# Last cross attention: score products for the maximum stream 128 key columns in place of 77

## The reference

```python
q = (x @ Wq + bq).reshape(B, N, NUM_HEADS, HEAD_DIM)      # 2 x 512 x 16 x 8
k = (y @ Wk + bk).reshape(B, M, NUM_HEADS, HEAD_DIM)      # 2 x 77 x 16 x 8
v = (y @ Wv + bv).reshape(B, M, NUM_HEADS, HEAD_DIM)
scores = jnp.einsum('bnhd,bmhd->bhnm', q, k) * scale
attn = jax.nn.softmax(scores, axis=-1)
out = jnp.einsum('bhnm,bmhd->bnhd', attn, v).reshape(B, N, IMAGE_DIM)
h = jax.nn.relu(out @ W1 + b1)
return h @ W2 + b2
```

## Time and profile before

| what | value |
|---|---|
| median of 3 runs | 844.75 us |
| the three runs | 837.37, 844.75, 848.48 us |
| the profiled execution | 845.99 us |
| its span in the trace | 843.9 us |
| mean granted TensorE clock | 0.805 |

### The profile page before, as it was taken

The page is one execution under the profiler, slowest core; times in us unless marked ns, Lnnn a source line. Parts: engine busy times, 40 slices in busy tenths (PEclk is TensorE's granted clock), DMA queues, the critical chain, the costliest instruction groups (busy, mean ns, idle before and its releaser), DMA issues. The chain is left out here.

```text
span 843.9 us, 9225 instructions
## 1 busy us (share of the span) xinstructions
PE 654.8 (78%) x3288; PEld 352.7 (42%) x3288; DVE 420.1 (50%) x803; ACT 376.0 (45%) x645; POOL 63.6 (8%) x56
## 2 busy tenths in 40 slices
PE   3089949999996866999999341899998424996798
PEld 2013313333433344899999211123332212434686
DVE  3087727677515645422211675857872513423555
ACT  3037726766660423634433121257888122543321
POOL 4100200110010000000000520000000120002100
PEclk9559959999996756899999665559999755557699
DMA  8405430650014052000000002000000054000000
GB/s 202 80 8 69 46 31 2 76 75 3 2 22 53 1 229 117 1 1 1 1 2 1 1 0 25 1 0 2 2 2 2 11 73 42 2 2 1 1 1 25
DMA packets 15979, 25.58 MB, mean 30 GB/s; under 512 B 2663, under 2 KB 10391, under 8 KB 15551
## 3 DMA queue, kind: packets, MB, share of 16 engines
q1 hardware_dynamic: 14572, 23.08, 15.5%
q10 hardware_dynamic: 1363, 1.93, 1.0%
HBM read 9.99 MB, written 0.52 MB: 12 GB/s over the span
## 5 line engine op out<-in xcount | busy, mean ns | idle before, releaser
L387 DVE TENSOR_REDUCE negmax<-ps 128x2 f32<-128x1024 f32 x96 | 114.5, 1221 | 65.6 <-PE ps L319 65.2
L428 ACT ACTIVATE probs<-ps 128x512 f32<-128x512 f32 x192 | 106.0, 599 | 51.0 <-PE ps L340 49.4
L387 DVE TENSOR_REDUCE negmax_q<-ps 128x2 f32<-128x1024 f32 x64 | 75.7, 1217 | 23.5 <-PE ps L319 23.5
L1353 PEld LDWEIGHTS ps<-wproj,hid 128*128 128x128 f32 x640 | 83.5, 191 | 6.9
L428 ACT ACTIVATE probs_q<-ps,score_scale 128x512 f32<-128x512 f32 x128 | 79.0, 686 | 16.1 <-PE ps L340 15.9
L1353 PE MATMUL ps<-wproj,hid 128*128 128x128 f32 x640 | 83.8, 274 | 0.0
L1382 ACT ACTIVATE hid<-ps 128x512 f32<-128x512 f32 x80 | 47.6, 597 | 69.8 <-PE ps L665 69.8
L665 PE MATMUL ps<-h,wfc 128*128 128x512 f32 x240 | 76.9, 432 | 0.0
L319 PE MATMUL ps<-k_gated,q_gated 72*128 72x512 bf16 x128 | 44.4, 434 | 28.1 <-DMA k_gated<-parts 22.0
L319 PE MATMUL ps<-ks_q,qs_q 72*128 72x512 bf16 x128 | 47.4, 460 | 11.8 <-PEq L1571 8.6
L1449 DVE SCALAR_TENSOR_TENSOR x_tok<-ps,comb,x_tok 128x128 f32<-128x128 f32 x64 | 18.0, 344 | 77.0 <-PE ps L1353 77.0
(11 more groups left out here) (312 smaller groups left out, 902.6 us busy)
## 6 DMA issues: line engine op xcount, KB each, us to landing
q_wide<-parts SPq DMA_DIRECT2D x12, 256.0 KB, 5.8
k_wide<-parts SPq DMA_DIRECT2D x12, 256.0 KB, 7.5
wfc<-in_L_ffn_Wfc_dram SPq DMA_DIRECT2D x1, 2560.0 KB, 9.5
wproj<-in_L_ffn_Wproj_dram SPq DMA_DIRECT2D x1, 2560.0 KB, 15.2
q_gated<-parts SPq DMA_DIRECT2D x12, 128.0 KB
k_gated<-parts SPq DMA_DIRECT2D x12, 128.0 KB
qs_x<-parts_x SPq DMA_DIRECT2D x12, 128.0 KB
w<-in_L_ffn_W_dram SPq DMA_DIRECT2D x1, 1024.0 KB, 17.0
```

The costliest lines, as they stand in the source:

```text
L387: nc.vector.tensor_reduce(maxima, scores, AX.X, ALU.max, negate=True).then_inc(self.a_max_done, 1)
L428: nc.scalar.activation(self.probs[0:size, g % self.P_SLOTS, :], ps[0:size, self.B_BANK + g % self.B_SLOTS, :], ACT.Exp, scale=scale).then_ ...
L1353: last = nc.tensor.matmul(K.ps[:, y_bank(g), i * P:(i + 1) * P], hid[:, m % SLOTS, i * P:(i + 1) * P], wproj[:, FT * e + f, :], start=(f = ...
```

## The change

A job gets two new fields, `span` and `span0`: how many key columns a matmul of step A streams, and from which column of the stack. For every job but those of the last cross attention they are what was there before. There, `span` is 128; `span0` is 0 for batch entry 0 and 154 - 128 = 26 for entry 1. Each A matmul so streams 128 neighbouring key columns that hold the job's own 77 and 51 of the other batch entry, and four heads fill a PSUM bank of 512. The reduction reads the job's own 77 of each 128 (from column 0, or from column 51), so the maxima are the same. Steps M, B, V, E and T, the order, and the buffers are not touched.

```diff
@@ class Job
         self.keys = sum(n for _, n in key_tiles)
+        self.span, self.span0 = self.keys, k0
@@ Attention.tensor, step A
-                            ps[:, bank, c * job.keys:(c + 1) * job.keys], job.q[0:job.rows, h, q0:q0 + P],
-                            job.k[0:job.rows, h, job.k0:job.k0 + job.keys], start=True, stop=True,
+                            ps[:, bank, c * job.span:(c + 1) * job.span], job.q[0:job.rows, h, q0:q0 + P],
+                            job.k[0:job.rows, h, job.span0:job.span0 + job.span], start=True, stop=True,
                             skip_group_check=True)
@@ Attention.vector, step A
-                scores = ps[:, bank:bank + 2, 0:len(heads[0]) * job.keys]
+                scores = ps[:, bank:bank + 2, 0:len(heads[0]) * job.span]
...
-                    scores = scores.rearrange("p b (j k) -> p b j k", k=job.keys)
+                    own = job.k0 - job.span0
+                    scores = scores.rearrange("p b (j k) -> p b j k", k=job.span)[:, :, :, own:own + job.keys]
@@ cross_attention_heads
+    for job in jobs:
+        job.span, job.span0 = P, (NB * NK - P) * job.b
```

## The result

The changed kernel takes 848.16 us (median of 20 runs, 841.34 to 852.35), the one before 844.61 us (20 runs beside them, 837.37 to 848.48). The ratio is 1.0047, with a 95% interval of 1.0026 to 1.0069: slower by 3.55 us in the medians (2 to 6 us by the interval), clear of noise and far inside 2%.

The account below looks back on a forecast made before the run. The last cross attention was taken as DMA-bound up to 712.9 us, then PE-bound at 1.2 GHz. Ten A blocks at 0.34 us add 3.4 to 844.75, giving 848.2, stated as 848 us; range 840 to 854.

Parts of the forecast that it names:

- The price of one matmul: Step A, last cross attention: 0.107 us between starts at 128 columns, 0.0425 us dearer each, 0.34 us per block.
- Where the blocks lie: Of step A's 16 blocks, six before the first B cost nothing, ten behind it 0.34 us each: 3.4 us.
- the cover: Before the first B: PE's 6.20 us wait for small DMAs queued behind larger `qs_x` loads, hiding six A blocks.
- The reduction: VectorE's read of step A's scores in pieces: unchanged at 0.79 us, upper bound 1.217 us.
- Behind the stage: After the last cross attention: only its start moves, 3.4 us later; clock edges up to 2 us either way.
- The clock: Rival: longer streams raise the clock inside the last cross attention, saving 15 to 18 us, about 832 us; chance 7%.
- The sum: Whole kernel: 844.75 + 3.4 = 848.2 us as the median, +0.4%.

Follow-up runs that it names:

- split kernels: 128 columns only in the first six A blocks, or only in the last ten, against the kernel before: ratios 1.0005 and 1.0032, stages 63.6 and 66.9 us.
- the pieces alone: Against the kernel before: 77 columns per A matmul, but the heads' scores 128 apart in PSUM, so VectorE reads 77 of every 128; ratio 0.9979.

## Why the prediction was right

*The price of one matmul.* Taken as 0.107 us between starts, from the pace at 77 and at 512 columns; it is 0.107 in the changed kernel, and 102 columns lie on the same line.

*Where the blocks lie.* Ten blocks at 0.34 us were to cost 3.4 us and six nothing. The split kernels give 3.3 and 0.0 us, and the changed kernel's stage 3.47, of which 0.15 lie ahead of the first B (13.43 us instead of 13.28) and 3.32 behind it. The reason named for the cover was half right. The small DMAs do wait for the large loads, and doubling the streams shows the wait to be some 6 us deep; but SyncE's queue isn't where they wait. Three A blocks lie ahead of the first M and not the two that I counted; M came 2.85 us behind the first A for 2.37 before, 0.48 later, inside the 0.4 to 0.7 allowed.

*The reduction.* Taken as unchanged, from a strided operation of the same length as a packed one; the pieces alone gave a stage of 63.67 against 63.60 us.

*Behind the stage.* I allowed 2 us either way for the edges of the clock. From the transposes of `tok_a` to the end of the last product it was 77.1 us before and after (763.21 to 840.36, and 760.40 to 837.52), so nothing came of it in these two executions.

*The clock.* It did not rise, as forecast, and doubling the streams didn't raise it. The argument for that was weak: that the streams lengthen a part already without gaps. I had listed the 128 rows in V of the stage before (here 77) and drew nothing from them. The kernels with V show what else counts: with the same columns and the same 1.94 us, 128 contracted partitions in V in place of 77 let the clock rise. The price set on that rival, 15 to 18 us, was somewhat high: 12.8 us, since behind the rise PE waits for VectorE and ScalarE and the stage needs 26.9 us from there.

*The sum.* 848.2 us was worked out and 848.16 measured; a ratio of 1.0041 (848.2 over 844.75) and 1.0047 measured, interval 1.0026 to 1.0069. That the two times agree to 0.04 us is chance, with runs 11 us apart; that the stage grew by 3.47 us for a forecast of 3.4 is not.

## What to carry to other kernels

Where one engine is busy without a gap in a stage, as here at the lower clock, widening its streams costs their own time and no more; where it waits for another, as here at the upper clock, the cost can vanish in the wait. Count only the instructions behind the last wait that isn't the engine's own, and take the price from the distance between starts at two sizes, not from a record's length.

If a stage runs without gaps at the lower clock, more of the same streams need not raise it, and letting its products contract all partitions may. Padding the contraction with zeroed partitions took no time in V and gave back 1.4% of the whole; padding the streamed columns cost 0.5%.

Where runs of one kernel differ by more than the effect, measure the stage from its own first instruction.

## What was not expected of the hardware

- A contraction over 128 partitions, 51 of them zeros, takes the time of one over 77 (a V of 1.94 us in both at the lower clock), and with it the granted clock went from 0.50 to 1.00 in a stage where it had stayed at 0.50 for over 60 us. It did so in all four such kernels, 23.8 to 31.0 us behind the first A.
- The clock of identical work in the attention before rose some 12 us apart in two executions, and the stage that follows began 5.4 us sooner for it, as much as half of the 11 us between runs of one kernel.
- Small DMAs issued from SyncE still kept the first B waiting until the large loads issued from ScalarE's queue were through: 8.7 us from the issue (698.8) to the start of B (707.48).
- A VectorE reduction over 77 of every 128 PSUM columns is as fast as over a packed run (0.799 us at the median, 0.800 before).
